# Slab loads by GpSimd, and the first block of a state-space phase with two convolutions on VectorE and its gate projections inside the units

## The reference

```python
xn = _layernorm(x)
x = x + _L0_attn_ref(xn, ...) + _L0_ffn_ref(xn, ...)   # differential attention, 16 heads; 8 experts, top 2, and a shared one
xn = _layernorm(x)
x = x + _L1_attn_ref(xn, ...) + _L1_ffn_ref(xn, ...)   # state-space block; three layers of weights +-1
```

```python
xz = x @ in_proj_w.T                 # 256 -> 1024; xc, z = halves of 512 channels
xs = silu(conv(xc) + conv_b)         # four taps over time, channel by channel
x_dbl = xs @ x_proj_w.T              # 16 for the step size, 16 for B, 16 for C
dt = softplus(x_dbl[:16] @ dt_proj_w.T + dt_proj_b)
h[t] = exp(dt*A) * h[t-1] + dt*B*xs  # 512 channels x 16 states, over time
y = (sum over states of h*C + xs*D_skip) * silu(z)
out = y @ out_proj_w.T
```

## Time and profile before

| | us |
|---|---|
| median of 3 runs | 3686.15 |
| lowest, highest | 3685.03, 3688.43 |
| profiled execution, its time | 3683.52 |
| its span, first to last instruction | 3681.7 |
| TensorE busy | 3381.3 |
| VectorE busy | 2735.0 |
| ScalarE busy | 2217.7 |
| GpSimd busy | 1501.7 |

### The profile page before, as it was taken

The page is one execution under the profiler, slowest core; times in us unless marked ns, Lnnn a source line. Parts: engine busy times, 40 slices in busy tenths (PEclk is TensorE's granted clock), DMA queues, the critical chain, the costliest instruction groups (busy, mean ns, idle before and its releaser), DMA issues. The chain is left out here.

```text
span 3681.7 us, 61156 instructions
## 1 busy us (share of the span) xinstructions
PE 3381.3 (92%) x20658; PEld 1448.4 (39%) x20671; DVE 2735.0 (74%) x4434; ACT 2217.7 (60%) x3461; POOL 1501.7 (41%) x1849
## 2 busy tenths in 40 slices
PE   8996999989999999999999999677998998989987
PEld 5563666643333333333333333342333333333332
DVE  4653223458888888888888888256888888888888
ACT  3331221137777777777777777637667766667663
POOL 2212000013333333323323333206778777777776
PEclk9997999989999999999999999888999999999988
DMA  4443111111111111111111010131212212222221
GB/s 152 143 138 98 46 44 44 41 37 39 48 41 30 32 34 33 33 33 33 30 33 31 28 29 25 37 120 58 73 60 79 66 65 71 65 75 70 64 72 52
DMA packets 159225, 211.69 MB, mean 57 GB/s; under 512 B 30659, under 2 KB 106699, under 8 KB 158939
## 3 DMA queue, kind: packets, MB, share of 16 engines
q1 hardware_dynamic: 142042, 174.47, 15.5%
q10 hardware_dynamic: 10752, 16.78, 1.4%
q0 software_dynamic: 6144, 16.79, 1.4%
HBM read 154.48 MB, written 52.69 MB: 56 GB/s over the span
## 5 line engine op out<-in xcount | busy, mean ns | idle before, releaser
L1331 DVE TENSOR_REDUCE pmax<-psR 128x1 f32<-128x512 f32 (+3 forms) x2170 | 1318.3, 669 | 162.0 <-PE psR L1383 94.5
L1277 ACT ACTIVATE prob<-psS 128x1024 f32<-128x1024 f32 (+3 forms) x1280 | 1099.9, 905 | 339.7 <-PE psS L1436 331.9
L2091 POOL TENSOR_TENSOR hc<-h_d,crep 128x512 f32<-128x512 f32 x512 | 649.0, 1272 | 253.6 <-DVE h_d L2305 203.3
L1383 PE MATMUL psR<-kslab,qslab 48*128 48x512 bf16 (+3 forms) x2480 | 677.3, 353 | 45.1 <-DVE pmax L1331 20.3
L1436 PE MATMUL psS<-qslab,kslab 51*128 51x512 bf16 (+3 forms) x2560 | 643.6, 352 | 6.8 <-ACT prob L1277 4.4
L1451 PE MATMUL psVo<-prob,vaug 128*32 128x512 f32 (+3 forms) x5120 | 625.4, 544 | 0.9 <-ACT ov L1281 0.9
L1209 POOL TENSOR_SCALAR_AFFINE_SELECT prob<-prob 128x256 f32<-128x256 f32 (+1 forms) x512 | 209.0, 421 | 779.6 <-ACT prob L1277 779.2
L2305 DVE TENSOR_TENSOR_SCAN h_d<-a,state,psU 128x512 f32<-128x512 f32 x384 | 489.3, 1274 | 0.0
L2295 DVE TENSOR_TENSOR psU<-dtx,psX 128x512 f32<-128x512 f32 x512 | 356.1, 695 | 165.6 <-PE psX L2449 102.7
L1383 PEld LDWEIGHTS psR<-kslab,qslab 48*128 48x128 bf16 x2480 | 185.3, 94 | 720.3 <-DVE pmax L1331 532.5
L2213 ACT ACTIVATE a<-dt,a_neg 128x512 f32<-128x512 f32 x512 | 364.7, 720 | 54.4 <-DVE h_d L2305 53.1
(11 more groups left out here) (289 smaller groups left out, 4852.8 us busy)
## 6 DMA issues: line engine op xcount, KB each, us to landing
crep<-c_rows_d SPq DMA_DIRECT2D x256, 256.0 KB, 3.2
x_e<-rows_d SPq DMA_DIRECT2D x72, 128.0 KB, 2.0
y_d<-y SPq DMA_DIRECT2D x72, 128.0 KB, 1.7
q_d<-parts SPq DMA_DIRECT2D x48, 128.0 KB, 2.4
k_d<-parts SPq DMA_DIRECT2D x48, 128.0 KB, 4.4
qslab<-q_d SPq DMA_DIRECT2D x64, 96.0 KB
kslab<-k_d SPq DMA_DIRECT2D x64, 96.0 KB
x<-in_L_attn_x_dram SPq DMA_DIRECT2D x8, 512.0 KB, 6.1
```

Source lines behind the costliest of these rows:

```text
L1277: act.activation(prob[g % BUFS][:, :, off:BLK], psS[g % 2][:, :, off:BLK], ACT.Exp).then_inc(prob_ready, 1)
L1331: dve.tensor_reduce(pmax[:, a].rearrange("p i c -> p (i c)")[:, lo:lo + (count - 1) * NEXT + 1:NEXT], psR[at % BANKS][:, 0:count * w].rear ...
L1383: ins = pe.matmul(dst[:, m * w:(m + 1) * w], qslab[u][rows, i * P:(i + 1) * P], kslab[u][rows, ch * BLK:ch * BLK + w], start=(m == 0), sto ...
L2091: pool.tensor_tensor(hc[:, g % CR], h[:, g % HR], crep[:, g // PAIR % SPR], ALU.mult).then_inc(hc_ready, 1)
```

## The change

Expert phase: the 24 slab transfers and the six of qz are issued by GpSimd, behind its memsets; SyncE goes from the lambda loads straight to the steps. The ones of all four slabs are filled there (eight memsets). One semaphore, `early_in`, counts all 30 transfers, and TensorE waits for all of them before the first max_product. Attention phase: no memsets and no `masks`. State-space phase: in the prologue the order becomes xz0, xz1, cv0, xz3, xz2, cv2; the convolutions of channel groups 1 and 3 are made by VectorE with one tensor_scalar and three scalar_tensor_tensor each; the gate projections of block 0 become items `z0` at units 4 to 7 of block 0; its l1 items 2 and 3 go from units 4 and 6 to 8 and 9, and the xz items 0 to 3 of block 1 from 5, 7, 12, 16 to 12, 14, 15, 16. silu_gate(0) goes to unit 27, copy_x(0) to the start, and SyncE's load_x(1) to behind spread_c(5).

The diff, cut to its core:

```diff
@@ phase_experts, SyncE
-            sp.wait_ge(early_made, 2 * SLABS + 2 + CREDIT)
-            for n in range(SLABS):
-                for a in range(2):
...
-            for a in range(2):
...
             steps(sp, step, 0, RT + 3)
@@ phase_experts, GpSimd
-            for n in range(SLABS):
+            for n in range(RING):
                 for a in range(2):
                     c.mark(pool.memset(kslabs[n][HALF * a + 32:HALF * a + HALF, :], 1.0))
             c.wait()
+            for n in range(SLABS):
+                for a in range(2):
+                    row, lo = 2 * n + a, HALF * a
+                    for at_, count, part in ((0, 3, 0), (3, 2, 1), (5, 1, 2)):
+                        pool.dma_start(qslabs[n][lo + at_ * HD:lo + (at_ + count) * HD, :],
+                                       q_rows[row, part].unsqueeze(0).to_broadcast([count, HD, T])).then_inc(early_in, 16)
+                    for at_, count in ((0, 3), (3, 2), (5, 1)):
+                        pool.dma_start(kslabs[n][lo + at_ * HD:lo + (at_ + count) * HD, :],
+                                       k_rows[row, 0:count].rearrange("x d t -> (x d) t")).then_inc(early_in, 16)
             for a in range(2):
                 c.after(pool.memset(qz[a][:], 0.0))
+            for a in range(2):
...
@@ phase_experts, TensorE, max_product
-                        pe.wait_ge(slab_in[0], 192 + CREDIT)
-                        pe.wait_ge(pad_in, 96 + CREDIT)
-                        pe.wait_ge(early_made, 2 * SLABS + 6 + CREDIT)
+                        pe.wait_ge(early_in, 384 + 96)
+                        pe.wait_ge(early_made, 2 * RING + 6 + CREDIT)
@@ phase_attention, SyncE and GpSimd
-            sp.wait_ge(masks, 2 * (RING - SLABS) + CREDIT)
-            for u in range(SLABS, RING):
-                for a in range(2):
-                    c.mark(pool.memset(kslab[u][HALF * a + 32:HALF * a + HALF, :], 1.0))
-            c.wait()
@@ phase_state_space
+        CONVS = [("xz", 0), ("xz", 1), ("cv", 0), ("xz", 3), ("xz", 2), ("cv", 2)]
+        BY_HAND = (1, 3)
+        HAND = NTAP * len(BY_HAND)
+        INPUTS = CONVS + [("xd", 0)] + [("dt", c) for c in range(PAIR)]
@@ pieces
-            for f, at in enumerate((0, 2, 4, 6, 10, 13, 15, 17)):
+            for f, at in enumerate((0, 2, 4, 6, 10, 13, 15, 17) if blk else (0, 2, 8, 9, 10, 13, 15, 17)):
                 put("l1", f, at, [4])
+            if blk == 0:
+                for n in range(CT):
+                    put("z0", CT + n, 4 + n, [KD])
-                for e, at in enumerate((5, 7, 12, 16, 49, 51, 53, 55)):
+                for e, at in enumerate(((5, 7, 12, 16) if blk else (12, 14, 15, 16)) + (49, 51, 53, 55)):
@@ SyncE
-            freed(0, "xz", ET - 1)
-            sp.wait_ge(xl_ready, 2 + CREDIT)
-            load_x(1)
             store_c(0)
             for k in range(SPREADS):
                 spread_c(k)
+                if step == 5 and blk == 0:
+                    sp.wait_ge(xl_ready, HAND + 2 + CREDIT)
+                    freed(0, "z0", ET - 1)
+                    load_x(1)
@@ ScalarE
             def silu_conv(nb, pair):
+                if nb == 0:
+                    act.wait_ge(xl_ready, HAND + CREDIT)
-            for kind, e in INPUTS:
+            copy_x(0)
+            for kind, e in CONVS:
...
             for pair in range(2):
                 silu_conv(0, pair)
-            silu_gate(0)
-            copy_x(0)
+                    if t == 27 and blk == 0:
+                        silu_gate(0)
@@ VectorE
+            c_hand = Chain(dve, xl_ready)
+            for c in BY_HAND:
+                s, n = PLACE[(0, "xz", c)]
+                dve.wait_ge(free[s], n + CREDIT)
+                dve.wait_ge(halo_ready, 1 + CREDIT)
+                dst = xs[:, input_tile(0, c)]
+                c_hand.after(dve.tensor_scalar(dst, xc[:, c, 0:BLK], conv_w[:, c, 0:1], vec[:, 0, c:c + 1],
+                                               ALU.mult, ALU.add))
+                for tap in range(1, NTAP):
+                    c_hand.after(dve.scalar_tensor_tensor(out=dst, in0=xc[:, c, tap:tap + BLK],
+                                                          scalar=conv_w[:, c, tap:tap + 1], in1=dst,
+                                                          op0=ALU.mult, op1=ALU.add))
             for k in range(KD):
                 cut_x(0, k)
```

More of the change, by code:

```diff
@@ L649, in phase_experts @@
         BIG = 1024
-        SLABS = 2
+        SLABS, RING = 2, 4
         kslabs, qslabs = keep["kslabs"], keep["qslabs"]
@@ L722, in _ @@
         def _(sp):
-            for s in sems + slab_in:
+            for s in sems:
                 sp.sem_inc(s, CREDIT)
@@ L743, in _ @@
                 sp.dma_start(lam_in[:, w, :], io[name].partition_broadcast(P)).then_inc(lam_load, 16)
+            steps(sp, step, 0, RT + 3)
+            for s in range(2):
+                sp.wait_ge(y_out[s], 16 * (RT // 2) + CREDIT)
+        @block.gpsimd
+        def _(pool):
+            c = Chain(pool, early_made)
+            c.wait()
+            for n in range(RING):
+                for a in range(2):
+                    c.mark(pool.memset(kslabs[n][HALF * a + 32:HALF * a + HALF, :], 1.0))
+            c.wait()
             q_rows = dram["q"].rearrange("b n x d t -> (b n) x d t")
             k_rows = dram["k"].rearrange("b n x d t -> (b n) x d t")
-            sp.wait_ge(early_made, 2 * SLABS + 2 + CREDIT)
             for n in range(SLABS):
@@ L758, in _ @@
                 for at_, count, part in ((0, 3, 0), (3, 2, 1), (5, 1, 2)):
-                    sp.dma_start(qz[a][lo + at_ * HD:lo + (at_ + count) * HD, :],
-                                 q_rows[row, part].unsqueeze(0).to_broadcast([count, HD, T])).then_inc(pad_in, 16)
-            steps(sp, step, 0, RT + 3)
-            for s in range(2):
-                sp.wait_ge(y_out[s], 16 * (RT // 2) + CREDIT)
-            for n in range(SLABS):
[L765 to L769, removed]
-            c.wait()
-            for n in range(SLABS):
-                for a in range(2):
-                    c.mark(pool.memset(kslabs[n][HALF * a + 32:HALF * a + HALF, :], 1.0))
-            c.wait()
-            for a in range(2):
-                c.after(pool.memset(qz[a][:], 0.0))
+                    pool.dma_start(qz[a][lo + at_ * HD:lo + (at_ + count) * HD, :],
+                                   q_rows[row, part].unsqueeze(0).to_broadcast([count, HD, T])).then_inc(early_in, 16)
             c.after(pool.memset(ident_m[:], 0.0))
@@ L999, in phase_attention @@
         pmax = keep["pmax"]
-        kslab = keep["kslabs"] + [sb(f"kslab{u}", [P, T], BF16) for u in range(SLABS, RING)]
+        kslab = keep["kslabs"]
         qslab = keep["qslabs"] + [sb(f"qslab{u}", [P, T], BF16) for u in range(SLABS, RING)]
@@ L1026, in phase_attention @@
         lam_step = sem("b_lam_step")
-        masks = sem("b_masks")
         setup = sem("b_setup")
-        slab_in = keep["early_in"] + [sem(f"b_slab_in{u}") for u in range(SLABS, RING)]
+        slab_in = [sem(f"b_slab_in{u}") for u in range(RING)]
         mrow_in = sem("b_mrow_in")
@@ L2535, in build @@
                 side = lambda name, shape, dt: early.enter_context(nc.sbuf_tensor(name, shape, dt, side="right"))
-                keep["kslabs"] = [side(f"kslab{u}", [P, T], BF16) for u in range(2)]
+                keep["kslabs"] = [side(f"kslab{u}", [P, T], BF16) for u in range(4)]
                 keep["qslabs"] = [side(f"qslab{u}", [P, T], BF16) for u in range(2)]
@@ L2543, in build @@
                 keep["pmax"] = side("pmax", [P, 2, ST_T, BPB], F32)
-                keep["early_in"] = [early.enter_context(nc.semaphore(f"b_slab_in{u}")) for u in range(2)]
+                keep["early_in"] = early.enter_context(nc.semaphore("m_early_in"))
                 phase_experts(nc, io, keep, dram)
```

42 lines of the change are left out of this document (19 added, 23 removed).

## The result

| | before | after |
|---|---|---|
| median of the runs, us | 3685.77 | 3646.16 |
| lowest to highest | 3685.03 to 3688.43 | 3644.96 to 3652.44 |
| profiled execution | 3683.52 | 3652.44 |
| its span | 3681.7 | 3650.7 |

The kernel before was run again beside the changed one, so its median is not quite the 3686.15 us of the table ahead. The ratio after to before is 0.9896 [0.9882, 0.991]: 39.6 us faster, where 35.3 were forecast. The two profiled executions are only 31.1 us apart. That of before is 2.2 us under its median and that of after 6.3 over its own, so the profile shows where most of the gain is, but not all of its size.

What follows compares the result with a forecast made beforehand. TensorE was busy 92% of the span, but the change touches three short places where it stands still or works ahead. 23.6 + 1.9 + 12.8 - 3.0 = 35.3 us off the 3686.15 us median gave 3651, range 3642 to 3662.

Steps and rivals of the forecast that it cites:

- Part 1 and 2: Expert phase start: x_e stall gone and gate products faster, 23.6 us; attention start: memsets moved away, 1.9 us.
- psM wait for the slabs: Expert phase: a TensorE wait for the slab transfers, listed as showing the forecast wrong; no size given.
- Part 3: State-space prologue: TensorE loses four xz and two cv items, 13.7 us, less 0.9 of waiting; net 12.8 us.
- all of that moves forward by 12.8 us: State-space prologue: xd, the splits, step sizes and first scan all come 12.8 us earlier.
- rival (a): First block: gates don't fit, all 6.9 us shows, or lower clock slows xd and step sizes; 3659 us, chance 0.13.
- sign of being wrong: State-space prologue: a lower clock level during xd, listed among what would show the forecast wrong.
- Part 4: First state-space block: moved gate projections add 6.9 us of TensorE, mostly into slack; loss 3.0 us, bounds 0 to 7.
- the middle of 1.8 and 4.1: First block, units 4 to 20: loss 1.8 us without bank waits, 4.1 with all of them; 3.0 taken.
- the lower level may fall otherwise in several blocks: State-space blocks: low clock level could fall differently in several at once, where the forecast would be most wrong; no size.
- (b): Expert phase: transfers still collide in the DMA engines, tile loads land late, gain there only 11.0 us; 3663 us, chance 0.07.
- (c): Early score products: GpSimd's 30 transfers not done in time, kernel slower, 3738 us at 12 us each; chance 0.01.
- (d): Expert phase: another SyncE wait still holds load(1) until the slabs are in; 3674 us, chance 0.02.

Runs made afterwards that it cites:

- after_again: The changed kernel itself, unaltered, run and profiled once more: 3648.99 us, ratio 0.9903 to the kernel before.
- slabs_sync: The changed kernel with the 30 slab and padded transfers issued by SyncE, in three batches between the tile loads: 3658.40 us, ratio 0.9927.
- early_sign: The changed kernel with VectorE copying a block's second r tile out of PSUM at that block's last unit, not in the next block: 3627.03 us, ratio 0.9836.
- early_sign_2: The changed kernel with the earlier copy of the second r tile, run again for comparison on one chip: 3625.48 us, ratio 0.984.
- only_state: The kernel before with the state-space part of the change alone: 3670.47 us, ratio 0.9959.
- gates_back: The changed kernel with the four gate projections back in the prologue and block 0's old unit plan: 3652.57 us, ratio 0.9906.
- convs_back: The changed kernel with convolutions 1 and 3 back on TensorE in the prologue: 3652.15 us, ratio 0.9903.
- only_early: The kernel before with only the expert and attention parts of the change, old state-space phase: 3659.67 us, ratio 0.9930.

## Why the prediction was right

**Part 1 and 2, 25.5 us: right, term by term.** The first column gives 25.7 and 25.7, and the kernel with these parts alone 25.4. The whole 22 us stall went, the gate products fell to 1.98 us, and the gain at the first scores was 2.0 us more than at the end of the expert phase (last copy of y 23.4 us earlier, first scores 25.5, in times of the span). GpSimd's 30 transfers at 0.54 to 0.65 us each were half of the 1.3 that the bound allowed, the last went out at 345.3 where 372 was reckoned, and no psM wait for the slabs appeared.

**Part 3, 12.8 us forecast, 10.3 and 11.0 measured: its removal was right, its last step was not.** xd starts 32.41 - 20.38 = 12.0 us nearer to the first input product, and 12.7 in after_again, as the first table load does (12.0 and 12.7, a sign that the prediction named), with the foreseen wait in front of the last convolution (0.77 for 0.9). The term that failed is "all of that moves forward by 12.8 us": it took xd's 3.60 us over from the earlier trace rows, and in both profiles of after xd ran at 5.30. The prediction held this only as part of rival (a) and as a sign of being wrong. Over all profiles, xd takes 5.30 us in five of the six that have this short prologue (after, after_again, slabs_sync, early_sign, early_sign_2), where the granted clock falls to 0.5 within xd, and 3.60 in only_state. It takes 3.60 to 3.63 in all seven others: the old prologue, products put back, or the gaps filled. So it goes with the short prologue and its idle time, but not in every execution; what decides it is open.

**Part 4, 3.0 us forecast, 4.6 and 4.3 measured: the place right, the size not.** Against before, block 0 has lost 2.0 us at unit 10, 3.8 at unit 20 and 4.6 from unit 27 on; nothing changes after that. That is near the 4.1 us with all bank waits that the working had for units 4 to 20, and a little more in the units behind. Taking the middle of 1.8 and 4.1 was the wrong choice: the waits are all there, 0.80 us for sz's bank and VectorE's 2.33 behind the first gate item. That item was forecast at 3.4 us and took 3.62. No decay wait came at unit 30.

**So in the stages that they touch, parts 3 and 4 together gave 5.7 and 6.7 us, not 9.8**, and the halves of the edit differ: by the same stages the convolutions on VectorE brought about 3, the move of the gates brought nothing (from a gain of 0.2 to a loss of 1.4, over four profiles), and gates come cheap only in the gaps of the prologue. These are single profiles against single profiles, and the medians of gates_back and convs_back don't settle it.

**The sum came out right by more than its terms.** The three stages that the change touches give 31.4 us (after) and 32.4 (after_again), where the terms gave 35.3; the medians give 39.6, 36.1 (after_again) and 35.8 (with the later stalls taken out of both). That the medians come so near to 35.3 is in part luck. If the profiled stages are typical, the rest of 4 to 8 us lies in the two stages that the change doesn't touch. In the last one, before and only_early took 1032.1 and 1032.4 us. The four profiles with exactly the new state-space code took 1031.2 (after), 1027.4, 1027.1 and 1027.2 (after_again, only_state, slabs_sync). Over this stage the granted clock is at 0.5 for 125 us in the first two, for 107 in after and for 100 in the last three. The prediction named this at its end (the lower level may fall otherwise in several blocks) and put no number on it. That a longer low stretch goes with a longer block is shown by after and after_again, in four blocks. Why it should fall better behind the new prologue is not shown, and that it does on average rests on four profiles against two.

**The rivals.** (a) is half true: xd did run at the lower clock (1.7 us, not 4 with the step sizes), and 4.6 of the 6.9 us showed. (Its own sum takes 4 us where its words, 3.6 + 2.0, make 5.6.) In the profiled execution this makes the state-space part worth 5.7 us in place of 9.8; the median shows nothing of it. (b) is refuted. From landing 5.9 us at most, no wait came back, and slabs_sync shows what it would have been with SyncE still carrying the slabs: about 10 us of the 23.7 lost. The Trainium skill, DMA: Bandwidth & Descriptors, Issuing engines are not separate DMA queues, holds that another issuing engine saves only the time of starting the transfers. This case's trace is in line with it in that tile loads among the slabs land later whoever issues these: the one at 333.97 took 5.9 us, 3.9 over the median. But what was saved is 22 us, more than the 16.9 us of issuing, because the loads behind them were also freed from the wait for the memsets ahead (313.6 to 321.3 before). (c) and (d) did not occur.

## What to carry to other kernels

Look for the in-order queue in which urgent transfers stand behind ones that nobody needs for a long time, and give those to an engine that is idle: it took away a whole stall here, and spreading them among the urgent ones on the same queue left 10 us of it. Issue the urgent ones early as well: beside bulk transfers they landed two to three times later. Work moved from a prologue into a loop is paid again wherever the loop's engine has no slack yet; put it first into the gaps of the prologue itself (the stage times show this, the medians don't). And before tuning a small stage, ask the list of waits for one that repeats in every block: 5.5 us seven times, from one line issued two units too late, was worth as much as a whole edit of this kind.

## What the runs showed of the hardware

- A direct transfer issued by GpSimd occupies it for 0.577 to 0.652 us (qslab), less than the indirect one of 0.97 us, and lands in 3.2 us (2.2 to 4.4) while the tile loads run beside it.
- A float32 tensor_scalar of 512 columns that reads SBUF takes 0.55 us on VectorE, and a scalar_tensor_tensor 0.75, no faster than the 0.73 for one that reads PSUM.
- The same instructions in the same place get full clock in one execution and half in another: xd 5.30 us in five profiles of the short prologue and 3.60 in a sixth (only_state), block 4 of one program 142.7 or 146.6 us. Two medians of four runs of the changed kernel differ by 2.8 us, and six runs of one program spread over 16 us.
